# Attention on one core: paired maxima, one PSUM bank for the small TensorE jobs, rotation by DMA, normalisation on VectorE

## The reference, cut to what matters

```python
q = jax.nn.elu(q) + 1.0          # 16 heads of 8 numbers
k = jax.nn.elu(k) + 1.0
q = _apply_rope(q, sin, cos)     # out[even] = x[even]*cos - x[odd]*sin ; out[odd] = x[even]*sin + x[odd]*cos
k = _apply_rope(k, sin, cos)
attn = jnp.einsum('bhnd,bhmd->bhnm', q, k) * scale
attn = jax.nn.softmax(attn, axis=-1)
attn_out = jnp.einsum('bhnm,bhmd->bhnd', attn, v)
```

## Time and profile before

| | before |
|---|---|
| median of 3 runs | 1349.93 us (1349.86 to 1350.73) |
| profiled execution, time | 1361.09 us |
| profiled execution, span | 1359.3 us |
| PE / DVE / ACT / POOL busy | 1119.0 / 1078.1 / 944.2 / 839.2 us |
| share of the span | 82 / 79 / 69 / 62 % |
| mean granted TensorE clock | 0.917 |

### The profile page before, as it was taken

One profiled execution on the slowest core, in us unless ns is written; L12 is line 12 of the kernel. 1 busy time (PEld: TensorE's weight loads), 2 busy tenths in 40 slices (PEclk: granted clock), 3 DMA queues, 4 the chain that ended last, 5 costly groups with the idle time before them and its releaser, 6 DMA issues. The chain is left out here.

```text
span 1359.3 us, 22331 instructions
## 1 busy us (share of the span) xinstructions
PE 1119.0 (82%) x6568; PEld 478.2 (35%) x6568; DVE 1078.1 (79%) x2483; ACT 944.2 (69%) x1748; POOL 839.2 (62%) x1145
## 2 busy tenths in 40 slices
PE   2599999999999999999999998971799897777710
PEld 0122222232232222332322222221588685556510
DVE  2589999999999999999999999623667575898644
ACT  1028888887887887887888787860699784776511
POOL 5244366566676876877777775545477436885555
PEclk9559999999999999999999999985899997999965
DMA  2462241241242341342332331002234533444312
GB/s 61 89 173 65 60 103 50 65 111 50 73 119 57 96 117 44 93 98 64 89 87 72 87 88 47 19 20 93 84 122 144 172 122 103 128 140 130 86 32 76
DMA packets 104009, 119.89 MB, mean 88 GB/s; under 512 B 13217, under 2 KB 80965, under 8 KB 103621
## 3 DMA queue, kind: packets, MB, share of 16 engines
q1 hardware_dynamic: 93728, 97.55, 26.5%
q0 software_dynamic: 8192, 16.79, 4.5%
q10 hardware_dynamic: 1968, 4.13, 0.8%
HBM read 58.91 MB, written 59.51 MB: 87 GB/s over the span
## 5 line engine op out<-in xcount | busy, mean ns | idle before, releaser
L922 DVE TENSOR_REDUCE MX<-psS 128x1 f32<-128x512 f32 x1024 | 651.2, 679 | 67.1 <-PE psS L423 61.1
L678 ACT ACTIVATE PR<-psST 128x512 f32<-128x512 f32 x986 | 536.7, 599 | 133.6 <-PE psST L411 124.9
L423 PE MATMUL psS<-KS,QS 48*128 48x512 bf16 x1024 | 362.4, 401 | 33.7 <-DMA KS<-scratch_parts 18.5
L411 PE MATMUL psST<-QS,KS 51*128 51x512 bf16 x986 | 335.7, 388 | 24.5 <-ACT PR L678 8.5
L437 PE MATMUL psPV<-PR,V 128*32 128x512 f32 x2048 | 276.8, 613 | 7.4 <-ACT OT L592 2.2
L411 PEld LDWEIGHTS psST<-QS,KS 51*128 51x128 bf16 x986 | 77.5, 93 | 382.2 <-ACT PR L678 337.4
L1707 POOL DMA_INDIRECT GOT<-scratch_y,FROM x128 | 129.3, 1010 | 38.3 <-issue 35.9
L423 PEld LDWEIGHTS psS<-KS,QS 48*128 48x128 bf16 x1024 | 84.9, 93 | 88.9 <-DVE MX L922 62.7
L1033 POOL DMA_INDIRECT scratch_x<-XN,POSI x96 | 95.4, 994 | 26.7 <-issue 26.6
L1382 PE MATMUL psH<-XH,WS 128*128 128x512 f32 x184 | 83.2, 452 | 16.9 <-ACT XH L1434 6.8
L1384 PE MATMUL psH<-XH,WS 128*128 128x512 f32 x184 | 75.7, 411 | 0.0
(11 more groups left out here) (173 smaller groups left out, 2004.8 us busy)
## 6 DMA issues: line engine op xcount, KB each, us to landing
scratch_parts<-PT SPq DMA_DIRECT2D x192, 128.0 KB
QS<-scratch_parts SPq DMA_DIRECT2D x64, 192.0 KB, 3.5
KS<-scratch_parts SPq DMA_DIRECT2D x64, 192.0 KB, 4.4
XR<-scratch_x SPq DMA_DIRECT2D x46, 256.0 KB
scratch_y<-YR SPq DMA_DIRECT2D x46, 256.0 KB
scratch_x<-ZERO SPq DMA_DIRECT2D x18, 256.0 KB
X<-in_x SPq DMA_DIRECT2D x16, 256.0 KB, 5.0
scratch_turned<-XT SPq DMA_DIRECT2D x16, 256.0 KB, 4.5
```

What stands on the lines that cost most here:

```text
L411: nc.tensor.matmul(bank(st_banks(t), k)[:], KS[t.par][rows, h // 2, kc * P:(kc + 1) * P], QS[t.par][rows, h // 2, :], start=True, stop=Tru ...
L423: nc.tensor.matmul(bank(psS, k)[:], QS[b.par][rows, h // 2, qc * P:(qc + 1) * P], KS[b.par][rows, h // 2, :], start=True, stop=True).then_ ...
L678: nc.scalar.activation(PR[:, s % 2, j, :], bank(st_banks(t), k)[:], ACT.Exp, scale=SCALE).then_inc(st_exp, 1)
L922: nc.vector.tensor_reduce(out=MX[:, qc, h:h + 1], in_=bank(psS, k)[:], axis=AX.X, op=ALU.max).then_inc(s_max, 1)
```

## The change

It has five parts.

1. The maxima: `psS` becomes two pairs of banks. TensorE writes two tiles (two heads, same rows) into a pair, and VectorE takes both maxima by one instruction, 128x2 out of 128x1024, behind the second. A pair waits for the instruction two pairs before it.
2. With four banks for that, two for `psST` and one for `psPV`, one is left: `psM` is a single bank, and each small TensorE job waits for the reader of the job just before it.
3. The swap of the rotation leaves TensorE: SyncE copies `EL` to `RES` with even and odd partitions exchanged (`turn`, two DMAs for q, two for k), the sine has the signs in it, and the sine product moves from VectorE to GpSimd (`rotate`). The jobs `Rq` and `Rk` are gone.
4. The normalisation of x moves from GpSimd to VectorE, one instruction at each of the places (12,0), (12,2), (13,0), (13,2).
5. Places are shifted: ScalarE does its small jobs of slot s (all but the `OT` copy) behind the first exponential of slot s+1 instead of behind the last of slot s; elu is at (4,1) and (6,1) instead of (2,3) and (3,3); the k projection is in slot 4, `O3` in slot 6, `mT1` in slot 1; SyncE stores the maxima between the second and the third parts; GpSimd's order is changed; in the last main iteration the transposed tiles have six banks instead of five.

```diff
-        psS = [es.enter_context(nc.psum_tensor(f"psS{i}", [P, N], F32)) for i in range(S_BANKS)]
+        psS = [es.enter_context(nc.psum_tensor(f"psS{i}", [P, 2, N], F32)) for i in range(S_PAIRS)]
-        psM = [es.enter_context(nc.psum_tensor(f"psM{i}", [P, N], F32)) for i in range(2)]
+        psM = es.enter_context(nc.psum_tensor("psM", [P, N], F32))
...
-        MISC = ["xT", "q", "k", "mT1", "O3", "Rq", "Rk", "O0", "lepeT", "mT0", "O1", "vT", "xT2", "V",
+        MISC = ["xT", "mT1", "q", "k", "O3", "O0", "lepeT", "mT0", "O1", "vT", "xT2", "V",
                 "O2", "lg"]
...
             n = MISC.index(use)
-            for back in range(2, 2 * len(MISC), 2):
+            for back in range(1, 2 * len(MISC)):
...
+            def turn(b, w):
+                sp.wait_ge(qk_elu[w], b.done(1, 1))
...
+                for odd in range(2):
+                    sp.dma_start(RES[odd::2, w, :], EL[1 - odd::2, w, :]).then_inc(turned[w], 16)
...
-                if due(before := b.done(TILES, tile_before(psS, k) + 1)):
-                    pe.wait_ge(s_max, before)
+                pair = k // 2
+                if j % 2 == 0:
+                    if due(before := b.done(TILES // 2, pair - S_PAIRS + 1)):
+                        pe.wait_ge(s_max, before)
...
-                if s in (5, 6) and prep.live:
-                    w = s - 5
-                    use = ("Rq", "Rk")[w]
-                    misc_freed(pe, t, use)
-                    pe.wait_ge(qk_elu[w], prep.done(1, 1))
-                    nc.tensor.matmul(misc_bank(use)[:], PERM[:], EL[:, w, :], start=True, stop=True).then_inc(rot_psum[w], 1)
...
-                    extra(t, s)
+                        if j == 0 and s > 0:
+                            extra(t, s - 1)
+                    out_copy(t, s)
...
-                if s in (2, 3) and j == 3 and prep.live:
-                    elu(prep, s - 2)
-                if s == 5 and j == 3 and prev.live:
+                if s in (4, 6) and j == 1 and prep.live:
+                    elu(prep, s // 6)
+                if s == 7 and j == 1 and prev.live:
                     normalise(prev, 3, "O3")
-                if s in (6, 7) and j == 0 and prep.live:
...
-                    nc.vector.tensor_tensor(RES[:, w, :], misc_bank(("Rq", "Rk")[w])[:], SIN[:],
-                                            ALU.mult).then_inc(rot_sin[w], 1)
...
+                if s in (12, 13) and j in (0, 2) and far.live:
+                    qc = 2 * (s - 12) + j // 2
...
+                    nc.vector.tensor_scalar(XN[:, qc, :], X[:, far.number() * QC + qc, :], MV0[:, qc, 0:1],
+                                            RS0[:, qc:qc + 1], ALU.subtract, ALU.mult).then_inc(xn_ready, 1)
...
-                        if nxt.live:
+                        if nxt.live and j % 2 == 1:
...
-                            nc.vector.tensor_reduce(out=MX[:, qc, h:h + 1], in_=bank(psS, k)[:], axis=AX.X,
-                                                    op=ALU.max).then_inc(s_max, 1)
+                            nc.vector.tensor_reduce(out=MX[:, qc, h:h + 2].unsqueeze(2), in_=psS[k // 2 % S_PAIRS][:],
+                                                    axis=AX.X, op=ALU.max).then_inc(s_max, 1)
...
+            def rotate(b, w):
+                pool.wait_ge(qk_elu[w], b.done(1, 1))
...
+                nc.gpsimd.tensor_tensor(ROT[:, w, :], EL[:, w, :], COS[:], ALU.mult).then_inc(rot_cos[w], 1)
+                pool.wait_ge(turned[w], b.done(32, 32))
+                nc.gpsimd.tensor_tensor(RES[:, w, :], RES[:, w, :], SIN[:], ALU.mult).then_inc(rot_sin[w], 1)
...
+                nc.gpsimd.tensor_tensor(ROT[:, w, :], ROT[:, w, :], RES[:, w, :], ALU.add).then_inc(rot_sum[w], 1)
```

More of the change, by code:

```diff
@@ L50 @@
 VW = 32
[L51 removed]
+ST_BANKS, S_PAIRS = 2, 2
 TILES = H * QC
@@ L96, in constant, with attention @@
         first += size
-def attention(nc, x_in, wqkvT, chan, ones, rope_cos, rope_sin, perm, ident, numbers, count, gate_wT, gate_b,
+def attention(nc, x_in, wqkvT, chan, ones, rope_cos, rope_sin, ident, numbers, count, gate_wT, gate_b,
               X, IDF, TAB, ZERO, BD, XN2, POS, POSI, WSEL, CW, BASE, CNT, XG, XTD, scattered, zero_filled, table, load_weights):
@@ L197, in attention @@
         qk_elu = [sem(f"qk_elu{w}") for w in range(2)]
-        rot_psum = [sem(f"rot_psum{w}") for w in range(2)]
+        turned = [sem(f"turned{w}") for w in range(2)]
         rot_cos = [sem(f"rot_cos{w}") for w in range(2)]
@@ L265, in misc_freed, with st_bank @@
                     return
-        def bank(banks, k):
-            return banks[1 if len(banks) == 3 and k == TILES - 1 else k % len(banks)]
         def st_banks(t):
[L274 to L280, removed]
+            if t.c == B - 1:
+                return [m[:] for m in psST] + [m[:, i, :] for m in psS for i in range(2)]
+            return [m[:] for m in psST]
+        def st_bank(t, k):
+            banks = st_banks(t)
+            return banks[k % len(banks)]
         def max_tile(s, j):
@@ L404, in scores_t @@
                 if len(psST) <= k < len(banks):
-                    pe.wait_ge(s_max, t.done(TILES, TILES))
-                elif due(before := t.done(TILES, tile_before(psST if k < len(psST) else banks, k) + 1)):
+                    pe.wait_ge(s_max, t.done(TILES // 2, TILES // 2))
+                elif due(before := t.done(TILES, k - (len(psST) if k < len(psST) else len(banks)) + 1)):
                     pe.wait_ge(st_exp, before)
                 rows = slice(SIDE * (h % 2), SIDE * (h % 2) + ROWS_ALL)
-                nc.tensor.matmul(bank(st_banks(t), k)[:], KS[t.par][rows, h // 2, kc * P:(kc + 1) * P],
+                nc.tensor.matmul(st_bank(t, k), KS[t.par][rows, h // 2, kc * P:(kc + 1) * P],
                                  QS[t.par][rows, h // 2, :], start=True, stop=True).then_inc(st_psum, 1)
@@ L643, in extra @@
                 old, p = t + (-2), paired(t)
-                if s == 13 and old.live:
+                if s == 12 and old.live:
                     act.wait_ge(xT2_psum, old.done(1, 1))
@@ L797, in gate @@
                 p, b = paired(t), t + (-3)
-                if place == (0, 3) and b.live:
+                if place == (0, 2) and b.live:
                     dve.wait_ge(lg_psum, b.done(1, 1))
@@ L982, in rsqrt @@
                 pool.wait_ge(eps, b.done(1, 1))
-                if due(before := b.done(1, 0)):
+                if due(before := b.done(per, 0)):
                     pool.wait_ge(free, before)
@@ L1030, in scatter @@
                 pool.wait_ge(xn2_ready, b.done(1, 1))
-                for qc in range(QC):
+                for qc in chunks:
                     at = POSI[:, p % 2, k, b.par * QC + qc:b.par * QC + qc + 1]
@@ L1070, in iteration @@
                         nc.gpsimd.tensor_tensor(RES[:, w, :], ROT[:, w, :], PT[:, w, 0, :], ALU.subtract).then_inc(resid[w], 1)
[L1071 to L1073 removed]
                 if far.live:
[L1075 to L1084 removed]
+                    rsqrt(far, MV0, VE0, RS0, aggr0, eps0, rstd0, xn_ready, QC)
+                if prep.live:
+                    last_part(prep, 0)
+                if out.live and out.c < B - 4 and t.c < B:
+                    scatter(out, 1, range(2))
+                if prep.live:
+                    last_part(prep, 1)
+                if out.live and out.c < B - 4 and t.c < B:
+                    scatter(out, 1, range(2, QC))
                 if prev.live:
@@ L1108, in iteration @@
                 if out.live and out.c < B - 4 and t.c >= B:
-                    scatter(out, 0)
-                    scatter(out, 1)
+                    scatter(out, 0, range(QC))
+                    scatter(out, 1, range(QC))
             everywhere(iteration)(pool)
@@ L1801, in host_constants @@
     sin = np.sin(angle.astype(np.float64)).astype(np.float32).T[freq]
-    perm = np.zeros((C, C), np.float32)
-    for j in range(0, C, 2):
-        perm[j + 1, j] = -1.0
-        perm[j, j + 1] = 1.0
+    sin = sin * np.where(np.arange(C) % 2 == 0, -1.0, 1.0).astype(np.float32)[:, None]
     e, i, m = np.arange(NE), np.arange(MOST_UNITS), np.arange(STEPS)
```

125 lines of the change are left out of this document (60 added, 65 removed).

## The result

The changed kernel takes 1364.53 us (median of 4 runs, 1362.82 to 1366.47), the kernel before 1350.33 us beside it (1349.86 to 1352.15): a ratio of 1.0101, 95% interval 1.0084 to 1.0118. It is slower by 14.2 us. Its profiled execution took 1366.0 us, span 1364.1 us, mean granted clock 0.932; that is only 4.9 us more than the profiled execution of before, which lay 11 us above its own median.

A forecast was written before the change was run, and what follows sets the result against it. VectorE and TensorE looked nearly full, VectorE fuller, with ScalarE's lags passed to TensorE. 5 x 1.5 - 6 x 0.1 + 4 x 0.9 - 3 + 2 = +9.5 on 1361.1 gave 1370.6, times 0.9918 1359 us; range 1318 to 1383.

The forecast's parts named there:

- The sum of +9.5 us: Whole kernel: changes by kind of iteration, first maxima iteration and start-up add 9.5 us to the profiled 1361.1, giving 1370.6.
- The pair at 1.20 and 1.12: VectorE's maxima: a paired instruction lasts 1.20 us and the next can start after 1.12, against 1.20 for two single ones.
- with waits: Maxima's saving: 4.8 us over 32 pairs against the 1.28 us that two take on average, waits included; pure work 2.3.
- VectorE idle 6 us or more before the pairs: Sign that the forecast is right: VectorE idles 6 us or more a batch ahead of the maxima instead of 2.5.
- Slots: The sixteen slots, costed one by one with engine lags handed on: 2.4 to 4.3 us each, 52.1 us together.
- The larger part: ScalarE's small jobs between exponentials 0 and 1 delay tile D: small TensorE job at 2.4 us, 2.9 and 3.1 in slots 10 and 13.
- The first maxima iteration: -3: From 48 to 98.7 us, without exponentials: pairs help, -2.3 - 1.4 + 1.0 and some waits, 3 us shorter.
- The rotation by DMA: hidden: Between k's elu and ScalarE's part in slot 9: the chain needs 6.9 of 7.8 us, so 0.9 us to spare.
- The median is 0.9918 of that execution: Conversion from profiled execution to the median of the runs: factor 0.9918 turns 1370.6 into 1359 us.
- The pairs pay: Rival: VectorE stays the bound and the locks hide behind it, 2 to 4 us a batch gained, 1290 to 1320; chance 0.16.
- The clock falls: Rival: more TensorE waits bring more stretches at 1.2 GHz, up to +15 us; 0.16 together with late rotation and dear pair.
- The rotation comes late: Rival: DMAs land over 4.4 us after issue and ScalarE waits in slot 9; 1385 at 6 us; shares 0.16.
- The pair costs two instructions: Rival: a paired maximum lasts 1.36 us, nothing saved and every reader 0.24 later, 1391 us; shares 0.16.

The follow-up runs named there:

- e4: The changed kernel, unchanged, measured again in a set where the kernel before takes 1329.97 us: 1340.57 us, ratio 1.0080.
- e0: The kernel before, unchanged, profiled a second time: profiled execution 1331.2 us beside a median of 1329.8 us.
- e1: The changed kernel with ScalarE's small jobs behind exponential 1 of the slot instead of exponential 0: 1332.97 us, 1.0025 of the kernel before.
- e2: The changed kernel with the pairing alone undone, one maximum instruction per score tile on the same four banks: 1333.75 us, 1.0033 of the kernel before.
- e3: The changed kernel with single maxima, three score banks and two banks for the small jobs: 1322.87 us, 0.9942 of the kernel before.
- e8: The changed kernel with VectorE's readers of the one bank ahead of the first pair in slots 7, 8, 9, 11, 15: 1351.63 us against 1349.83, 1.0016.
- e10: The changed kernel, pairs and one bank kept, with the edits of e1, e5, e8 and GpSimd's clamp between rsqrt and products: 1344.22 us against 1349.83, 0.9963.
- e5: The changed kernel with the first experts' weights loaded behind slot 2 of iteration 0 instead of ahead of slot 0: 1341.13 us, 1.0083 of the kernel before.
- e9: The kernel before with only the rotation by DMA and GpSimd's sine product added: 1340.94 us against 1349.83, 0.9937.
- e11: e10 with the pairing alone undone, single maxima on the same four banks: 1354.58 us against 1355.27 for the kernel before, 0.9983.
- e6: The changed kernel with GpSimd's clamp of exp(q) put ahead of the second normalisation: 1356.58 us, 1.0205 of the kernel before.

## Why the prediction was right, and where it was not

**Sign and size: right.** I forecast 1359, slower with 0.54, its own range 1353 to 1383; it is 1364.5. The sum of +9.5 us stood against the profiled execution, though, and there the difference is 4.9; that the median came out near the forecast is in part luck (see the factor below). By kind of iteration: plain was forecast at 52.5 and measured 51.8. Against before that is 0.8 more in the first set (51.8 against 51.0) and 1.3 more in e4 against e0 (forecast 1.5). With the gate: 54.1 forecast, 52.7 to 54.0 measured, 0.3 less than before (52.7 in e4 against 53.0 in e0; forecast 0.1 less). Early: 50.4 forecast, 50.1 to 51.2 measured, but the four together grew by 1.7 us and not by 3.6, since the first of them took 51.5 before. Start-up +2 forecast; the first score of batch 0 starts 2.4 us later. The stretch from the last `XT` copy to the last `OT` copy, for which the sum has no term but one gate iteration, grew by 1.8 us (3.0 in e4 against e0); no run takes it apart.

**The pair at 1.20 and 1.12: right.** 1.22, and two in a row take 2.36, so the second starts 1.14 behind. The pure saving was 2.3 to 2.4 us a batch (forecast 2.3); of the 4.8 "with waits" 0.7 is left. The 4.8 was misread to begin with: 1.28 is the busy time of two maxima (287.1 / 448 twice) without the idle time before them. Four normalisations take 1.4 us (forecast 1.0). They don't visibly hold up GpSimd: its operations of line 1114 take 0.46 us beside one of them and 0.45 otherwise.

**VectorE idle 6 us or more before the pairs: too high.** It is 4.2 us a batch.

**Slots: the rules held in most, not in slot 1.** In the iteration from 461.88, slots 0 to 15 last 2.7, 2.7, 3.4, 2.6, 4.7, 2.6, 3.6, 3.0, 3.0, 2.9, 3.5, 3.5, 3.1, 3.7, 3.0, 3.4. Slots 4, 10 and 13 were forecast at 4.3, 3.5 and 3.8. Slot 1 took 0.7 less than forecast, and most of the sum's excess is there. Tile D of slot 13 behind ScalarE's two jobs, as forecast:

```profile
500.15 0.60 ACT L684 ACTIVATE PR<-psST 128x512 f32<-128x512 f32 x1
500.63 0.82 ACT L640 ACTIVATE LP<-VT,CHAN 128x512 f32<-128x512 f32 x1
501.33 0.60 ACT L657 ACTIVATE XT<-psM 128x512 f32<-128x512 f32 x1
501.81 1.69 ACT L684 ACTIVATE PR<-psST 128x512 f32<-128x512 f32 x3
502.48 0.39 PE L418 MATMUL psST<-QS,KS 51*128 51x512 bf16 x1 [0.77 <-ACT PR L684]
```

**"The larger part" was ScalarE's: wrong.** Undoing ScalarE's position gains 7.6 us (e1), a second bank 10.9 us (e2 to e3), readers ahead of the pair some 9 (e8). The two locks are of like size, and e10 fits gains that add up. I had put the bank at 3 to 4 us a batch by the 0.4 to 0.5 us in eight slots; it is 0.6 in plain iterations and 1.8 with the gate. It may be that the small job waited for tile D anyway in many slots; this was not tried apart. The rule of the Trainium skill ("Perfetto Trace Analysis", Matmuls), that independent matmul groups should rotate through different PSUM banks, is borne out by e3 in its direction.

**"The first maxima iteration: -3": the step that failed.** Measured +0.2 (+2.2 in e4 against e0). ScalarE comes to the weights' loads sooner (they are issued at 88.3 us instead of 92.3), and they fall on the stack loads of batch 1, for which TensorE waits 5 to 7 us; with the weights out of the way the iteration lasts 46.1 us (e5). It is not the clock: the rows show 0.60 for this iteration and 0.50 before, but in both profiles, as in e5, the 512-column matmuls of the projections (L550, before L547) start 1.01 us apart in it, against 0.53 in the later iterations. My sum asked what waits in the iteration and not which transfer starts at its end. Nor is the shortening the pairs', as the sum had it: e9, with single maxima and the rotation by DMA, takes 46.3 us where e0 takes 49.7, and e11 with single maxima 47.1 against 47.0 in e10 with pairs. Only e5 against e2 (46.1 against 46.9) shows 0.8 of the 2.3 us that I gave them.

**The rotation by DMA: hidden, as forecast**, and dearer in my account than it is. 128 KB land in 2.0 us, not 3.5. GpSimd waits up to 1.5 us for them in five early iterations, 4.1 us in all, and never from 356 us on:

```profile
RES<-EL SPq DMA_DIRECT2D x64, 128.0 KB, 2.0
```

What I didn't see is that this part alone is worth 8.9 us (e9); it is the part that pays, and e3, which keeps it, has about the same ratio. So the other re-placements and the move of the normalisation are together about neutral; they were not tried apart.

**"The median is 0.9918 of that execution": wrong.** The factor belonged to one profiled execution: in e0 it is 1329.8 / 1331.2 = 0.9989, and so it is for the changed kernel. What made that execution 11 us long stays open: its two stretches at 1.2 GHz last 6.8 us together, and e0 has three without such a loss. The sum for the changed kernel's profiled execution, 1370.6, stands against 1366.0: an error of +5, which the factor's error of -10 turned into -5.5 at the median. That the two errors have opposite signs is luck.

**The rivals.** The pairs pay: no, single maxima are faster (e2), and in the repaired order there is no difference (e10, e11). The clock falls: no, it is 1.00 from 102 to 897 us. The rotation comes late: no, GpSimd doesn't wait for it in the main iterations. The pair costs two instructions: no, it lasts 1.22 us and not 1.36.

## What to carry to other kernels

One wide instruction in place of two saves little (here 0.07 us of 1.28), and only if its engine is what ends the slot. Otherwise waiting for both inputs takes the saving back, and every reader behind it is late by the second half. A resource given up for it (a bank here) must be priced by what waits for it in each kind of iteration. When the order of an engine changes, look also at the transfers that it issues sooner, and at the work that stands behind their issue. When a change bundles several parts, look for the one that pays by itself: here the rotation by DMA, which needs neither the pairs nor the single bank.

## What the runs showed that I had not expected

A stack load of 192 KB, one of eight that are issued together, lands after 5.3 us by themselves and after 12.2 us when 2.9 MB are issued on another queue 1 us behind the first loads of the keys (e5, e4). The same issues in the middle of a slot keep ScalarE from its exponentials for 2.44 us (e5). A copy from SBUF to SBUF of 128 KB lands in 2.0 us. On GpSimd the place of one 0.6 us instruction among in-order work is worth 16 us of the whole (e6).
